# A graph network on one core: node sums over two 64-node spans a group, and VectorE's first-step order

## The reference

```python
edge_attr = silu(edge_attr_raw @ enc_W + enc_b)
for _ in range(4):
    e_in = concatenate([edge_attr, x[src], x[dst]])
    e_upd = layernorm(silu(e_in @ eW1 + eb1) @ eW2 + eb2, eg, ebeta)
    edge_attr = edge_attr + e_upd
    agg = segment_sum(edge_attr, dst, num_segments=N)
    n_in = concatenate([x, agg])
    x = x + layernorm(silu(n_in @ nW1 + nb1) @ nW2 + nb2, ng, nbeta)
x = layernorm(x0 + x)
```

## Time and profile before

| | |
|---|---|
| median of three runs | 2531.08 us |
| profiled execution: its time, its span | 2536.36 us, 2534.5 us |
| TensorE busy | 2368.0 us, 93% |
| VectorE busy | 2215.5 us, 87% |
| ScalarE busy | 1914.2 us, 76% |
| GpSimd busy | 1619.3 us, 64% |
| granted TensorE clock, mean | 0.982 |
| chain that ended last | TensorE 49%, GpSimd 26%, issue 10%, VectorE 9%, DMA 5% |

### The profile page before, as it was taken

How to read it: one execution, slowest core, us unless ns; L and a number is a source line. 1 busy time by engine, 2 the same in 40 slices (tenths; PEclk the granted TensorE clock), 3 DMA queues, 4 the chain that set the end, 5 groups by cost and what they waited for, 6 DMA issues and landing times.

```text
span 2534.5 us, 82599 instructions
## 1 busy us (share of the span) xinstructions
PE 2368.0 (93%) x27988; PEld 1852.9 (73%) x27988; DVE 2215.5 (87%) x6127; ACT 1914.2 (76%) x5248; POOL 1619.3 (64%) x1588
## 2 busy tenths in 40 slices
PE   5799999999979999999988999999997999999995
PEld 2577777777747888888765787888874788888874
DVE  7699999999856999999965999999984799999997
ACT  3577777777547888888845888888864888888874
POOL 2677777777107777777605777777721777777750
PEclk9899999999999999999998999999999999999998
DMA  5566676776247888888726888888844677667740
GB/s 167 176 201 200 204 201 201 202 206 200 91 143 211 262 259 253 256 257 261 225 90 190 245 254 257 257 258 254 263 132 150 196 208 207 203 203 210 208 142 27
DMA packets 382921, 515.14 MB, mean 203 GB/s; under 512 B 58581, under 2 KB 256356, under 8 KB 382490
## 3 DMA queue, kind: packets, MB, share of 16 engines
q1 hardware_dynamic: 303572, 302.15, 37.1%
q0 software_dynamic: 75264, 205.62, 29.4%
q10 hardware_dynamic: 3654, 1.99, 0.3%
HBM read 390.48 MB, written 119.05 MB: 201 GB/s over the span
## 4 chain that ended last, share of the span: by engine, by line
PE 49%; POOL 26%; issue 10%; DVE 9%; DMA 5%; ACT 2%; DVEq 0%; ACTq 0%; SPq 0%; POOLq 0%
POOL arena L1646 26%; PE psum L1687 11%; PE psum L1714 8%; PE psum L1675 7%; DMA arena<-node_tables,idx_all 4%; PE psum L1745 4%; PE psum L1667 4%; PE psum L2138 3%; DVE arena L1942 2%; PE psum L1699 2%; PE psum L2177 2%; PE psum L2151 2%; PE psum L1726 2%; DVE arena L1962 1%; PE psum L1709 1%
## 5 line engine op out<-in xcount | busy, mean ns | idle before, releaser
L1646 POOL DMA_INDIRECT arena<-node_tables,idx_all x1568 | 1605.9, 1024 | 822.5 <-issue 445.4
L1811 ACT ACTIVATE arena<-psum 128x1024 f16<-128x1024 f32 x392 | 401.5, 1024 | 403.3 <-PE psum L1687 402.6
L1901 DVE SCALAR_TENSOR_TENSOR arena<-psum,arena 128x1024 f16<-128x1024 f32 x392 | 477.7, 1219 | 159.6 <-PE psum L1714 84.4
L1714 PE MATMUL psum<-w_hi,arena 128*128 128x128 f16 x6272 | 589.3, 219 | 3.9 <-DVE arena L1901 3.9
L1714 PE MATMUL psum<-w_lo,arena 128*128 128x128 f16 x3136 | 545.5, 219 | 0.0
L1714 PEld LDWEIGHTS psum<-w_hi,arena 128*128 128x128 f16 x6272 | 498.3, 98 | 17.0 <-DVE arena L1901 5.2
L1687 PE MATMUL psum<-arena,w_hi 128*128 128x512 f16 x1568 | 471.1, 382 | 2.6 <-ACT arena L1848 2.2
L1675 PE MATMUL psum<-ident,arena 128*128 128x128 f16 x6272 | 418.1, 220 | 36.3 <-DMA arena<-node_tables,idx_all 35.3
L1675 PEld LDWEIGHTS psum<-ident,arena 128*128 128x128 f16 x6272 | 380.5, 98 | 61.9 <-DMA arena<-node_tables,idx_all 53.8
L1824 ACT ACTIVATE arena<-psum 128x128 f32<-128x128 f32 x1568 | 413.8, 290 | 5.5 <-PE psum L1714 5.5
L1812 ACT ACTIVATE psum<-psum 128x1024 f32<-128x1024 f32 x392 | 399.1, 1018 | 0.0
(11 more groups left out here) (177 smaller groups left out, 3129.6 us busy)
## 6 DMA issues: line engine op xcount, KB each, us to landing
state<-arena SPq DMA_DIRECT2D x294, 256.0 KB
arena<-state SPq DMA_DIRECT2D x294, 256.0 KB
arena<-node_tables SPq DMA_DIRECT2D x784, 64.0 KB
arena<-matrices SPq DMA_DIRECT2D x294, 128.0 KB
node_tables<-arena SPq DMA_DIRECT2D x100, 256.0 KB, 2.2
arena<-node_tables,idx_all POOLq DMA_INDIRECT x1568
arena<-rel_rows SPq DMA_DIRECT2D x98, 128.0 KB
matrices<-arena SPq DMA_DIRECT2D x98, 128.0 KB
```

The source lines that it names most:

```text
L1646: pool.indirect_dma_start(out=rows[n % R][:, t, :], out_offset=None, in_=p_table, in_offset=bass.IndirectOffsetOnAxis(ap=idx_all[:, n % G1 ...
L1714: x = pe.matmul(ps_v(k2)[:, t * P:(t + 1) * P], h[k2][:, half, t * P:(t + 1) * P], w[:, half, :], start=False, stop=half == 1 and h is hl, ...
L1811: act.activation(hh[k2], ps_h(k2), ACT.Silu).then_inc(S("hh"), 1)
L1901: dve.scalar_tensor_tensor(hl[k2], ps_h(k2), 1.0, hh[k2], ALU.mult, ALU.subtract).then_inc(S("hl"), 1)
```

## The change

The node sums go over the two 64-node spans of a group's halves, which the first one-hot matrix already uses, instead of one 128-node window. `d_grp` is now counted from each half's own lowest node. The matrix `oh` becomes `narrow`: 64 columns a tile, 256 instead of 512 bytes a partition, in the second half of the old place, so that stores and loads of `both` carry 768 instead of 1024 bytes a partition. The matmuls of tiles 0 and 1 write columns 0 to 63 of `ps_a`, those of tiles 2 and 3 columns 64 to 127; the counts likewise. `window` loads two registers, from the new `half_at`; `add_window` makes two additions of 64 columns (2 x 64 in the first step), each at its own place. The halves' spans can overlap, so the second addition waits for the first by the semaphore `added`, which now counts two a group. In odd slots of the first step `low_new` moves behind root operation seven; in the later steps the order stays.

```diff
@@ -99,6 +99,7 @@
 half_win = sb("half_win", [1, 2, P], I32)
+half_at = sb("half_at", [1, 2, P], I32)
 half_low = sb("half_low", [P, 2], F32)
@@ -163,6 +164,7 @@
 oh = [x[:, 0:GE // 4].bitcast(F8) for x in both]
+narrow = [x[:, GE // 8:GE // 4].bitcast(F8) for x in both]
 oht = [x[:, GE // 4:GE // 2].bitcast(F8) for x in both]
@@ -526,7 +528,9 @@
     dve.wait_ge(SU("rel"), 1)
-    done2(dve.tensor_scalar(d_grp, d_grp, red[:, 0:1], 255.0, ALU.subtract, ALU.min))
+    for h in range(2):
+        done2(dve.tensor_scalar(d_grp[:, h * HALF_E:(h + 1) * HALF_E], d_grp[:, h * HALF_E:(h + 1) * HALF_E],
+                                half_low[:, h:h + 1], 255.0, ALU.subtract, ALU.min))
     dve.sem_inc(SU("grp"), 1)
@@ -542,7 +546,8 @@
     dve.wait_ge(SU("groupT"), 3)
-    dve.tensor_copy(win[0:1, 0:G2], psum[0:1, 0, 128:128 + G2]).then_inc(SU("cols"), 1)
+    dve.tensor_copy(win[0:1, 0:G2], psum[0:1, 0, 128:128 + G2])
+    dve.tensor_copy(half_at[0:1, :, 0:G2], psum[0:1, 0, 2 * P:4 * P].rearrange("a (h g) -> a h g", h=2)[:, :, 0:G2]).then_inc(SU("cols"), 1)
     dve.tensor_scalar(half_win[0:1, :, 0:G2], psum[0:1, 0, 2 * P:4 * P].rearrange("a (h g) -> a h g", h=2)[:, :, 0:G2], 2.0, None, ALU.mult).then_inc(SU("cols"), 1)
@@ -1536,9 +1541,9 @@
             dve.tensor_scalar(oht[n % R12], rel_w[k], part_cmp[:, :], None, ALU.is_equal, saturate=False).then_inc(Z("oht"), 1)
-            dve.tensor_tensor(oh[n % R12].rearrange("p (t n) -> p t n", t=TPG),
-                              node_iota[:, :].unsqueeze(1).to_broadcast([P, TPG, P]),
-                              rel_all[:, :, n:n + 1].to_broadcast([P, TPG, P]), ALU.is_equal, saturate=False).then_inc(Z("oh"), 1)
+            dve.tensor_tensor(narrow[n % R12].rearrange("p (t n) -> p t n", t=TPG),
+                              node_iota[:, 0:HALF_N].unsqueeze(1).to_broadcast([P, TPG, HALF_N]),
+                              rel_all[:, :, n:n + 1].to_broadcast([P, TPG, HALF_N]), ALU.is_equal, saturate=False).then_inc(Z("oh"), 1)
 
@@ -1579,7 +1584,7 @@
             sp.wait_ge(Z("oh"), n + 1)
-            sp.dma_start(matrices[n, :, :], both[n % R12]).then_inc(S(f"oh{n % R}"), 16)
+            sp.dma_start(matrices[n, :, GE // 8:], both[n % R12][:, GE // 8:]).then_inc(S(f"oh{n % R}"), 16)
 
@@ -1589,7 +1594,7 @@
             sp.wait_ge(S("sum"), n - R12 + 1)
-            sp.dma_start(both[n % R12], matrices[n % G1, :, :]).then_inc(S(f"oh{n % R}"), 16)
+            sp.dma_start(both[n % R12][:, GE // 8:], matrices[n % G1, :, GE // 8:]).then_inc(S(f"oh{n % R}"), 16)
 
@@ -1733,17 +1738,20 @@
             if n:
-                pe.wait_ge(S("added"), n)
+                pe.wait_ge(S("added"), 2 * n)
             if s == 0:
...
             fence(pe)
+            hot = narrow[n % R12].rearrange("p (t n) -> p t n", t=TPG)
             for t in range(TPG if s == 0 else 0):
-                pe.matmul(ps_a[:, P:2 * P], ones16[:, :], oh[n % R12][:, t * P:(t + 1) * P],
-                          start=t == 0, stop=t == TPG - 1, skip_group_check=True)
+                to = P + t // 2 * HALF_N
+                pe.matmul(ps_a[:, to:to + HALF_N], ones16[:, :], hot[:, t, :],
+                          start=t == 0, stop=t % 2 == 1, skip_group_check=True)
             for t in range(TPG):
+                to = t // 2 * HALF_N
                 for p in range(2):
-                    x = pe.matmul(ps_a[:, 0:P], st_out[n % R][:, p, t * P:(t + 1) * P], oh[n % R12][:, t * P:(t + 1) * P],
-                                  start=t == 0 and p == 0, stop=t == TPG - 1 and p == 1, skip_group_check=True)
+                    x = pe.matmul(ps_a[:, to:to + HALF_N], st_out[n % R][:, p, t * P:(t + 1) * P], hot[:, t, :],
+                                  start=t == 0 and p == 0 and s > 0, stop=t % 2 == 1 and p == 1, skip_group_check=True)
             x.then_inc(S("sum"), 1)
@@ -1788,7 +1796,7 @@
         node_output(2, nothing)
-        pe.wait_ge(S("added"), last + 1)
+        pe.wait_ge(S("added"), 2 * (last + 1))
         node_tables_of(0)
@@ -1965,26 +1973,28 @@
             if here(n):
-                return dve.value_load(win[0:1, n % G1:n % G1 + 1], min_val=0, max_val=N - P)
+                return [dve.value_load(half_at[0:1, h, n % G1:n % G1 + 1], min_val=0, max_val=N - HALF_N) for h in range(2)]
 
...
                 return
-            if n:
-                dve.wait_ge(S("added"), n)
             dve.wait_ge(S("sum"), n + 1)
-            if s == 0:
-                dve.tensor_tensor(agg_deg[:, :, ds(w, P)], agg_deg[:, :, ds(w, P)],
-                                  ps_a[:, 0:2 * P].rearrange("p (k f) -> p k f", k=2), ALU.add).then_inc(S("added"), 1)
-            else:
-                dve.tensor_tensor(agg[:, ds(w, P)], agg[:, ds(w, P)], ps_a[:, 0:P], ALU.add).then_inc(S("added"), 1)
+            for h in range(2):
+                if n or h:
+                    dve.wait_ge(S("added"), 2 * n + h)
+                at = ds(w[h], HALF_N)
+                if s == 0:
+                    sums = ps_a[:, 0:2 * P].rearrange("p (k f) -> p k f", k=2)[:, :, h * HALF_N:(h + 1) * HALF_N]
+                    dve.tensor_tensor(agg_deg[:, :, at], agg_deg[:, :, at], sums, ALU.add).then_inc(S("added"), 1)
+                else:
+                    dve.tensor_tensor(agg[:, at], agg[:, at], ps_a[:, h * HALF_N:(h + 1) * HALF_N], ALU.add).then_inc(S("added"), 1)
 
...
                 return
-            dve.wait_ge(S("added"), last + 1 if c == NCH - 1 else last - LAG - 3)
+            dve.wait_ge(S("added"), 2 * (last + 1 if c == NCH - 1 else last - LAG - 3))
             cols = slice(c * CW, (c + 1) * CW)
@@ -2003,9 +2013,13 @@
                 root(n - 3, 6, 7)
-                low_new(n - LAG - 2)
+                if s:
+                    low_new(n - LAG - 2)
                 root(n - 3, 7, 8)
-                add_old(n - LAG)
+                if s:
+                    add_old(n - LAG)
+                else:
+                    low_new(n - LAG - 2)
                 root(n - 3, 8, 9)
```

## The result

The changed kernel takes 2636.81 us (median of four runs, 2634.51 to 2641.5) beside 2529.49 us for the kernel before in the same session: 1.0426 times as long, 95% interval 1.0413 to 1.0439. It is slower, as forecast, but by 107 us and not by 61: 2637 lies outside the range of 2550 to 2620. The two profiled spans differ by 2632.7 - 2534.5 = 98.2 us.

A forecast was written before the change was run, and what follows sets the result against it. Gathers were taken to bound the later steps and VectorE the first, with VectorE becoming the limit in both. 43.6 + 9.4 + 7 + 1.3 = +61 us on the median 2531.1 gave 2592, rounded to 2590; range 2550 to 2620.

The forecast's parts named there:

- the sum for the later steps: Later steps: VectorE's pair of slots takes 10.67 us against gathers' 10.27; +43.6 us in three steps, shifts +9.4.
- the first step's +7: First step: the second load makes each odd slot 0.15 us longer, 45 of them: +7 us.
- What bounds the kernel before: Later steps: gathers' pace, TensorE just keeping up, VectorE 0.75 us per two groups in hand; first step: VectorE.
- 0 to -0.22 us a group: TensorE's eight sum matmuls a group, 64 columns instead of 128: this gain, taken as hidden, nothing in the loops.
- The second load: Head of later-step slots, VectorE's queue: loads run in series, +0.30 us odd to even slot, +0.26 even to odd.
- The second addition: Later steps, VectorE: second 64-column addition waits for the first; both hand on after 0.46 us instead of 0.20, +0.26 a group.
- additions and half one-hot cancel: First step, VectorE, per group: two additions instead of one +0.27 us, half one-hot -0.27 us.
- the load's lead: First step, odd slots: low half behind root operation seven starts the loads 0.48 us earlier, leaving +0.15 us a slot.
- Ends: Outside the loops: one more setup operation and copy +0.3 us, slots and sums behind the last groups +1 us.
- both hidden: Rival: queue overlaps the two loads, second addition runs without visible wait; pair 9.71 us, about 2485 us; chance 0.05.
- loads hidden: Rival: loads cost nothing, the addition's wait is paid; pair 10.11 us, about 2525 us; chance 0.11.
- Slow loads: Rival: each second load takes 0.59 us instead of 0.31; pair 11.23 us, about 2677 us; chance 0.08.

The follow-up runs named there:

- c8: The kernel before with one gather a group instead of four, its rows used four times: 2483.72 us, ratio 0.9809.
- c3: The changed kernel with one register load a slot and one addition of 128 columns, keeping the half one-hot matrix and narrow matmuls: 2498.62 us, ratio 0.9881.
- c5: The changed kernel with the first step's old order, the low half between root operations six and seven: 2670.59 us, ratio 1.0524.
- c4: The changed kernel with the second addition into its own tile at a fixed place, without wait or register address; both loads stay: 2578.14 us, ratio 1.0189.
- c1: The changed kernel with one register load a slot instead of two, both additions going to the first half's place: 2547.41 us, ratio 1.0071.
- c7: The changed kernel with one gather a group instead of four, its rows used four times: 2594.14 us, ratio 1.0251.
- c2: The changed kernel with both loads, but one addition of 128 columns instead of two of 64: 2550.1 us, ratio 1.0084.
- c6: The changed kernel with the first root operation written with two inputs, the constant from a tensor: 2632.71 us, ratio 1.0373.
- v3: The v1 kernel with the second addition of odd slots behind root operation two instead of one: 2502.83 us, ratio 0.9876.
- v1: The changed kernel reordered, same sums: both loads and the second addition of each group stand behind other work: 2513.46 us, ratio 0.9908.

## Why the prediction was wrong

The step that failed is the sum for the later steps, "Per step 44 x 10.67 = 469.5 us", and with it the first step's +7: each was made from undisturbed slots. The pair was mis-sized, 10.94 on the mean for 10.67; the cause was right. What the sum had at nothing were disturbances: operations held by gathers (12 us in the later steps, 10 in the first) and late register loads (9 us).

- **What bounds the kernel before** was right: with fewer gathers it is faster (c8). TensorE stood 0.2 us behind, closer than VectorE. The sums' matmuls came out at the far end of "0 to -0.22 us a group" (0.23 us for 0.45), and hidden, as forecast (c3).
- **The second load**, +0.30 and +0.26: L1909 follows L1919 by 0.89 and 0.86 us (medians of the later steps) for 0.60, +0.29 and +0.26. Right. The Trainium skill's floor of about 600 ns a load (DMA: Bandwidth & Descriptors, Latency and other measured facts) isn't borne out as a floor: 0.30 us is the median, and 0.6 us is met at some places (c5).
- **The second addition**, +0.26 a group: 0.349 + 0.138 - 0.195 = +0.29. Right within 0.03; c4 and c1 show its parts. By the overhead that the Trainium skill gives (Perfetto Trace Analysis, Optimizing Scalar/DVE Operations, about 125 ns) later steps would hardly have changed. The rows show 0.06 us for the bare extra operation and 0.22 for its wait and its address; the measurement decides.
- **The later steps**, +53 forecast with the shifts, +79.2 measured. The 26 us are 4 from the tight pair (10.70 for 10.67, 132 times), 12 from operations held by gathers (c7; 6 of them at the first two root operations) and 9 from slots in which the queue's loads come some 0.35 us later than usual (the excess of L1919 to L1909 over its median, 4.4 in even and 4.8 in odd slots). Both disturbances are in the kernel before as well: there the first two root operations take 6.7 us beyond their medians in the later steps, and in 13 of 264 slots the queue gets through its one load 0.2 to 0.4 us later than usual; but there VectorE has idle time at the end of the even slots that can take up such delays; how much it took was not measured. I had written that the pair came "from one pair of slots without disturbance", and added nothing for it.
- **The first step**, +7 forecast, +20.3 measured in its loop. That additions and half one-hot cancel, and +0.15 us for the load's lead, hold (L1919 to L1543 0.893 us for 0.745). Missing were the held root operation, 10.4 us (c7), and 0.02 us an addition, 2 us. Shifted by the additions by 0.29 us, L312 starts 0.55 us after a gather's start and is held to its end; no row of before shows L310 held in this step, though it is held in 17 slots of the later ones.
- **Ends**: -1.3 for +1.3.
- The last 9 of the 45 us between 2592 and 2637 are no part of the mechanism: medians differ by 107, profiled spans by 98, as the profiled execution of before lay above its median and the one of after just below.

Of the rivals, both hidden and loads hidden are out by c1 and c2. Slow loads don't make the result (10 of 574 in the later steps' stretch last over 0.4 us).

What stays open: why the queue's loads come 0.35 us late in some slots. It happens with a quarter of the gathers too, 8.2 us over the later steps instead of 9.2, so the gathers are not its cause. The traces show one thing more: all 23 late slots of c7 are among the 25 of the change (slots 27, 59 and 91 of the first later step, say, or 36 and 68: often 32 slots apart), and 20 of them are late in c5 and c6 too, whose first steps take another time. That points to the place in the program and not to the moment; what happens at these places was not tried.

## What to carry to other kernels

When an engine takes over as the limit, its disturbances, which the former limit's slack absorbed, come with it: price the loop by the mean of disturbed slots, not by the cleanest one (here 0.16 us of 10.9, beside 0.29 for one load that was added). A register load or a wait costs by its place in the queue: against one load and one addition (c3, ratio 0.9881), the second of each raises the ratio to 1.0426, 138 us, at the head of the slot and with the wait uncovered, but only to 0.9876 (v3) or 0.9908 (v1) behind running work, which is 0 to 7 us.

## What the runs showed of the hardware

- A small VectorE operation of one input (TENSOR_SCALAR, 128x8) that starts 0.53 us or more after the start of a gather of 0.946 us, and would end before it, ends with it: so did 940 of 940 in the traces of this case, within 10 ns. At 0.55 us it takes 0.39 us instead of 0.17, at 0.70 us 0.24. Started up to 0.51 us after, none of 1979 was held. With two inputs it isn't held (c6), without the gather neither (c7).
- The other way round, gathers last 0.946 us on the median, but in the kernel before a third of them last longer, up to 2.46; in c1 their mean in a stretch rises from 0.978 to 1.012 us, with VectorE in another phase to them. That VectorE's hand-over from one operation to the next near a gather's end causes it is a correlation only; no run set the phase on purpose.
- A register load lasts 0.30 us nearly always, but over 0.4 us in a quarter of the loads of one stretch (51 of 194 in c5).
- A wait on the address operation costs the address as well: between two additions of 64 columns 0.11 us for the semaphore (c1 against c4) and 0.11 for the address that stands behind it (the change against c1).
- Eight matmuls of 64 columns on TensorE follow each other at 29 ns, of 128 columns at 56 ns (granted clock 1.00, the 2.4 GHz level). The next matmul starts 0.23 instead of 0.45 us after their first, half the time for half the columns; from the first start to the last end they take 0.40 instead of 0.61 us.
